# Local attention of a two-layer perceiver kernel: score matmuls ahead of the value projections, and six PSUM banks for the value projections

## The reference, cut to what matters

```python
q = h @ q_w.T + q_b
k = h @ k_w.T + k_b
v = h @ v_w.T + v_b
ph = _phrase_states(h)              # running mean within chunks of 32 tokens
pk = ph @ pk_w.T + pk_b
pv = ph @ pv_w.T + pv_b
# scores of q against the earlier k, the best 16 of them kept; score of the
# previous token's k, and of the previous token's pk; one softmax over all
w = jax.nn.softmax(all_sc, axis=-1)
out = jnp.einsum('bsn,bsnd->bsd', w, all_v)
```

## Time and profile before

| what | value |
|---|---|
| median of 3 executions | 2631.66 us |
| lowest and highest of them | 2630.71 and 2636.94 us |
| the profiled execution, its own time | 2635.64 us |
| span of its trace, first to last instruction | 2633.8 us |
| granted TensorE clock, mean over the span | 0.940 of 2.4 GHz |
| `local1` in the trace | about 2454 to 2570 us |
| `ffn1` in the trace | 2570 us to the end |

### The profile page before, as it was taken

One profiled execution on the slowest core, in us unless ns is written; L12 is line 12 of the kernel. 1 busy time (PEld: TensorE's weight loads), 2 busy tenths in 40 slices (PEclk: granted clock), 3 DMA queues, 4 the chain that ended last, 5 costly groups with the idle time before them and its releaser, 6 DMA issues. The chain is left out here.

```text
span 2633.8 us, 57280 instructions
## 1 busy us (share of the span) xinstructions
PE 2308.7 (88%) x21679; PEld 1509.7 (57%) x21955; DVE 1812.0 (69%) x3358; ACT 1574.0 (60%) x2934; POOL 1125.1 (43%) x896
## 2 busy tenths in 40 slices
PE   5389999999999999996698699995799899996885
PEld 2245665666566656665345477772567676774442
DVE  3467877888788877775164599995777777763126
ACT  3246666666666666666135399983477677886103
POOL 2245666666666665555000000004367676655000
PEclk9599999999999999998899799997899999996887
DMA  4322243224322321111531499984533334222202
GB/s 131 94 75 75 74 117 90 73 76 120 88 70 74 104 76 40 40 37 27 220 117 54 168 364 362 362 303 160 163 118 117 111 119 133 87 89 66 92 0 82
DMA packets 256290, 314.08 MB, mean 119 GB/s; under 512 B 71424, under 2 KB 182912, under 8 KB 255120
## 3 DMA queue, kind: packets, MB, share of 16 engines
q1 hardware_dynamic: 252064, 302.28, 35.7%
q10 hardware_dynamic: 3312, 6.03, 0.6%
q0 software_dynamic: 640, 2.10, 0.3%
HBM read 226.56 MB, written 48.10 MB: 104 GB/s over the span
## 5 line engine op out<-in xcount | busy, mean ns | idle before, releaser
L606 POOL TENSOR_TENSOR a_plo<-a_p,a_phi 128x512 bf16<-128x512 f32 x272 | 315.8, 1161 | 340.3 <-ACT a_phi L662 339.6
L806 PE MATMUL ps<-w_hi,a_xhi 128*128 128x512 bf16 x1086 | 412.6, 380 | 6.3
L807 PE MATMUL ps<-w_lo,a_xhi 128*128 128x512 bf16 x1086 | 412.7, 380 | 0.3 <-issue 0.2
L808 PE MATMUL ps<-w_hi,a_xlo 128*128 128x512 bf16 x1071 | 406.9, 380 | 0.1
L1978 POOL TENSOR_TENSOR a_plo<-a_p,a_phi 128x512 bf16<-128x512 f32 x256 | 306.1, 1196 | 168.5 <-ACT a_phi L2015 159.4
L628 ACT ACTIVATE a_kraw<-ps 128x256 f32<-128x256 f32 x272 | 104.2, 383 | 357.1 <-PE ps L808 355.8
L2110 DVE CUSTOM_DVE_ANT_0 a_junk<-ps,a_biasrow 128x512 bf16<-128x512 f32 x256 | 175.9, 687 | 116.0 <-PE ps L2225 90.5
L685 DVE TENSOR_TENSOR a_v<-ps,a_v 128x256 bf16<-128x256 f32 x272 | 114.1, 420 | 160.9 <-ACT a_v L630 159.5
L2010 ACT ACTIVATE a_p<-ps,a_mcol 128x512 f32<-128x512 f32 x256 | 174.8, 683 | 77.5 <-PE ps L2243 72.0
L699 DVE SCALAR_TENSOR_TENSOR a_kraw<-a_kraw,a_rn 128x1024 f32<-128x1024 f32 (+1 forms) x80 | 156.6, 1957 | 77.6 <-POOL a_rn L565 77.5
L565 POOL TENSOR_TENSOR a_rn<-a_rn,a_power 128x16 f32<-128x16 f32 (+1 forms) x80 | 204.0, 2550 | 6.7
(11 more groups left out here) (438 smaller groups left out, 6807.8 us busy)
## 6 DMA issues: line engine op xcount, KB each, us to landing
e_wst<-in_L_ffn_W SPq DMA_DIRECT2D x46, 2048.0 KB, 10.0
a_xn<-in_ctx SPq DMA_DIRECT2D x16, 1024.0 KB, 5.6
a_ks<-a_khi SPq DMA_DIRECT2D x256, 64.0 KB, 2.0
a_ks<-a_klo SPq DMA_DIRECT2D x256, 64.0 KB, 2.0
a_ct<-in_ctxT SPq DMA_DIRECT2D x16, 1024.0 KB, 6.6
a_ks<-k1h_d SPq DMA_DIRECT2D x128, 128.0 KB, 2.5
k1h_d<-a_khi SPq DMA_DIRECT2D x64, 128.0 KB, 2.0
k1l_d<-a_klo SPq DMA_DIRECT2D x64, 128.0 KB, 1.7
```

The costliest lines, as they stand in the source:

```text
L606: pool.tensor_tensor(p_lo[:, m % 3, :], p32[:, m % 2, :], p_hi[:, m % 3, :], ALU.subtract)\
L806: pe.matmul(out, x_hi[:, c, tile], w_hi[:, c, g, :], start=(c == 0), stop=False)
L807: pe.matmul(out, x_hi[:, c, tile], w_lo[:, c, g, :], start=False, stop=False)
L808: last = pe.matmul(out, x_lo[:, c, tile], w_hi[:, c, g, :], start=False, stop=(c == C - 1))
```

## The change

In `local1` the score matmuls move ahead of the value projections in the order of PE. The value projections go through six banks in the order 2, 3, 6, 7, 4, 5, 2, 3, in place of two, so that only the last two tiles have to wait for a stored one. On DVE the eight copies of value tiles, which stood ahead of the softmax, are put into it in two groups: four behind the row maximum (`m_ready`), four behind the normalised weights (`w_ready`). ACT, SP and POOL have the same instructions in the same order as before. The number of matmuls and copies is the same.

```diff
+    def bank_v(n):
+        return (2, 3, 6, 7, 4, 5)[n % 6]
...
-            for n in range(2 * B):
+
+            def value(n):
                 k, b = n // B, n % B
                 dve.wait_ge(v_mm, n + 1)
-                dve.tensor_tensor(vv[:, k, b, :], ps[:, 6 + n % 2, :], br[:, k, :], ALU.add).then_inc(v_cp, 1)
+                dve.tensor_tensor(vv[:, k, b, :], ps[:, bank_v(n), :], br[:, k, :], ALU.add).then_inc(v_cp, 1)
+
             dve.wait_ge(s_mm, 2)
...
             dve.tensor_scalar(z[:, :, 2], z[:, :, 1], -1.0, None, ALU.mult).then_inc(m_ready, 1)
-
+            for n in range(4):
+                value(n)
             step(dve.tensor_tensor(r1[:], r2[:], sc[:], ALU.not_equal))
...
             dve.tensor_tensor(wt[:, 1], sh4, per_head(z[:, :, 6], B, P), ALU.mult).then_inc(w_ready, 1)
+            for n in range(4, 2 * B):
+                value(n)
             for b in range(B):
                 dve.wait_ge(o_mm, b + 1)
...
                 last.then_inc(f_mm, 1)
-            for n in range(2 * B):
-                k, b = n // B, n % B
-                if b == 0:
-                    pe.wait_ge(w_in[3 + k], 16)
-                if n >= 2:
-                    pe.wait_ge(v_cp, n - 1)
-                for c in range(C):
-                    last = pe.matmul(ps[:, 6 + n % 2, :], (HT, PT_)[k][:, c, b * P:(b + 1) * P], w[:, 3 + k, c, :],
-                                     start=(c == 0), stop=(c == C - 1))
-                last.then_inc(v_mm, 1)
             pe.wait_ge(f_cp, 3 * C)
...
                 last.then_inc(s_mm, 1)
+            for n in range(2 * B):
+                k, b = n // B, n % B
+                if b == 0:
+                    pe.wait_ge(w_in[3 + k], 16)
+                if n >= 6:
+                    pe.wait_ge(v_cp, n - 5)
+                for c in range(C):
+                    last = pe.matmul(ps[:, bank_v(n), :], (HT, PT_)[k][:, c, b * P:(b + 1) * P], w[:, 3 + k, c, :],
+                                     start=(c == 0), stop=(c == C - 1))
+                last.then_inc(v_mm, 1)
             for k in range(2):
                 pe.wait_ge(w_ready, k + 1)
```

## The result

The changed kernel takes 2618.6 us (median of 5, 2617.03 to 2621.61) against 2631.66 us before (5, 2630.31 to 2636.94). The ratio is 0.995, its interval 0.9937 to 0.9963: 9.7 to 16.6 us faster, 13.1 by the medians. The forecast was 14.1 us and 2617.5. Measured again later, beside other kernels, the ratio was 0.9952 (0.994 to 0.9965).

The account below looks back on a forecast made before the run. The stage was taken as bound by PE, then DVE alone, then PE again. 11.4 + 0.7 + 2.5 = 14.6 us, less 0.5 for the next stage, gave 14.1 and 2617.5 us; about 9 in 10 within 2612.5 to 2624.

Parts of the forecast that it names:

- The bubble: PE ahead of the scores, now waiting for ACT's last feature copy: a new idle time, taken as 1.0 us.
- Value tiles: Eight tiles on PE behind the scores, 3.43 us each, 27.47 in all, waiting for no weights or banks.
- DVE: Softmax and value copies beside PE's value tiles: weights ready at 2536.9, wanted at 2545.0, 8.1 us of slack, softmax hidden completely.
- before all is lost: Rival that the gain does not arrive: DVE's softmax late by 8.1 us before it costs anything, 14 before all is lost; chance 0.09.
- Start of the transposes: Transposes of the weights on PE start at 2545.0 instead of 2556.43: 11.4 us earlier.
- Clock of the tail: Transposes and products of `local1` at clock 1.00 instead of partly 0.50: saves 0.7 and 2.5 us, bounds 0 and 3.2.
- The rival that the clock drops at the transposes: Products begin at low clock: gain 7.8 to 12.1 us less 0.5, time 2620 to 2624, likeliest 2621; chance 0.09.
- The next stage: Clock at the onsets of dense work in the stage behind `local1`: 0.5 us taken off the gain, bounds 0 and 1.1.
- The rival in which the clock is lost in front of the long block: Clock drops at 2510, so scores and values run low: slower, at worst 2652 us; chance 0.02.
- The rival in which the measurement hides half: Part of the rival that the gain stays within 0.3%, 7.9 us: executions differ by up to 6.2 us; 2624 to 2631; chance 0.09.

Follow-up runs that it names:

- Experiment 5: Changed kernel with value tile 0 moved ahead of the scores, into the wait for the last feature copy: `local1` 100.27 us, ratio 0.9963 to the kernel before.
- experiment 1: Changed kernel with the value tiles through two banks (6 and 7) in place of six: `local1` 103.06 us, median 2614.9 us, ratio 0.9942 to before.
- Experiment 3: Changed kernel with all eight value copies between row maximum and weights, in place of four: `local1` 109.63 us, median 2626.15 us, ratio 0.9975 to before.
- experiment 2: Changed kernel's PE order and six banks, but DVE's eight value copies ahead of the softmax as before: `local1` 117.23 us, ratio 1.0007 to before.
- Experiment 4: Kernel before with 13 extra matmuls filling PE's idle time between scores and transposes: `local1` 113.01 us, ratio 0.9981 to before.
- 6: Changed kernel, value tile 0 ahead of the scores, transposes ahead of the last tile, each product waiting for its own tiles: `local1` 99.49 us, ratio 0.9957 to before.
- experiment 7: Changed kernel with 16 extra matmuls in PE's three idle times in `ffn1`: `ffn1` 61.13 us, median 2614.42 us, ratio 0.9949 to before.
- experiment 9: As Experiment 8, but with 20 extra matmuls in `ffn1` in place of 16: `ffn1` 59.38 us, median 2613.03 us, ratio 0.9925 to before.
- Experiment 8: Changed kernel with the edits of 6 and experiment 7 together: `local1` 98.94 us, `ffn1` 60.26 us, ratio 0.9936 to before.

## Why the prediction was right

Point by point, in the order of the prediction's steps:

1. *The bubble*: taken as 1.0. Without it the scores would have begun 0.21 ahead of ACT's last copy, as the value tiles did before (2509.22 against 2509.43, rows 2 and 4), at 2504.56 - 0.21 = 2504.35; they began at 2505.30: 0.95. Experiment 5 gives 1.02 for it.
2. *Value tiles*: no wait, 27.46 us against 27.47. The banks count for 1.6 of the gain (experiment 1); the forecast had only said that none would be waited for.
3. *DVE*: slack of 8.1 us forecast and 8.1 found. Experiment 3 used it up and paid beyond it; experiment 2 shows that without this half of the change the softmax is not hidden. DVE was idle in front of tiles 2, 3, 5, 6 and 7 and of no other, as said. One figure on this slack was wrong, the 14 us of delay "before all is lost": in experiment 3 the first weights came 13.7 us later than in the changed kernel (95.55 us behind the first statistics, against 81.83), and 6.4 us of the gain were left.
4. *Start of the transposes*: 11.4 us earlier. From first statistics to transposes it is 2556.43 - 2454.43 = 102.00 before and 2540.01 - 2449.46 = 90.55 after: 11.45.
5. *Clock of the tail*: 3.2 forecast. Products begin 1.78 us after the transposes (2.66 before, 1.9 forecast) and take 2547.90 + 1.02 - 2541.79 = 7.13 (9.57 before, 7.0 forecast): 0.88 + 2.44 = 3.3. Experiment 4 gives 3.05 with the old order, so it is the clock. The rival that the clock drops at the transposes did not come true: the transposes and 0.74 us of waiting were passed at 1.00. The Trainium skill's rule (TensorE: Matmul & The Clock Gate, Part 4) that transposes do not count as activity for the clock is not tested by this run: its 1.78 us without an ordinary matmul are shorter than the 1.86 us of plain idle time that did no harm in the earlier trace rows. The earlier trace rows speak against the rule, and so does a stretch shown below this list.
6. *The next stage*: I took 0.5 off with a bound of 1.1, and the profiled pair has +1.14. It is clock: the two onsets ran low for 1.55 and 0.77 us longer, and half of the sum is 1.16. This is the term that was mis-sized. I had thought a low onset of 4.9 us the longest, and there were 5.40 and 5.04; and I took the first onset before for 3.4 from the earlier trace rows, where it is 3.85, since two records are missing at its start. Whether the longer onsets are a cost of the change stays open. Its two traces, 64.45 and 64.11, are the longest of the nine with an unedited `ffn1`; the other seven had 62.86 to 63.66, and among them are experiments 1, 3, 5 and 6, whose `local1` is shorter than before too. Experiments 7 and 9 bear out that the clock is what the stage pays for: with PE kept at work it took 61.13 and 59.38, at least 1.7 and 3.5 us under the shortest of those.

The stretch that bears on the transposes (point 5) is of the trace before, and follows the first fall of the earlier trace rows; the timeline of PE and two of its microseconds:

```profile
1400.20 5.27 PE L933 MATMUL ps<-identf,s_q 128*128 128x128 f32 x32
1403.00:1404.00 1.00, 1.00 (x8) 1.00 (x7) 0.00 (x0) 0.83 (x2) 0.00 (x0) 0.75 0.94 352
1404.00:1405.00 1.00, 1.00 (x12) 1.00 (x11) 0.00 (x0) 1.00 (x3) 0.00 (x0) 1.00 1.02 369
```

From 1399.22 to 1405.47 PE did nothing but float32 transposes (the eight of the earlier trace rows and these 32). The clock fell at about 1400.1 and rose again at about 1403.5, while they ran. For the bfloat16 transposes of `ffn1` the runs decide nothing: experiment 9 passed 3.07 us of them and their waits at 1.00, and in 7 and 8 the fall came among them.

The rival in which the clock is lost in front of the long block did not happen either. It stood at 1.00 over the values (2510 to 2540), behind a wait of 0.78 us, and experiment 1 had a further wait of 1.33 us with two banks, its 45.4 us from the scores to the products at 1.00 as well.

Terms 4 and 5, 11.45 and 3.32, make up the measured 14.77, where 14.6 was forecast. Less 1.14 in `ffn1` this is 13.6 us; the medians say 13.1, the forecast was 14.1. The interval of the times, 9.7 to 16.6 us, is too wide to test a term of 0.5 us, so that the total came close says nothing for that term. The rival in which the measurement hides half did not happen in the medians, but the profiled pair alone, 18.6 us, would have been misleading: 5 us of it lie in a stage that did not change.

## What to carry to other kernels

When an engine stands idle behind a chain on another one, look for work on it that the chain does not need, and move it behind the chain's input; and then move its consumer's instructions out of the chain on the other engine as well, into a place where there is slack. The first order alone gave nothing (experiment 2). The second alone was not run; by the program it could not work here, since PE would wait at value tile 6 for a copy that stands behind scores which it has not made. Count the clock with it: an idle time of 12 us ahead of short dense work cost 3 us more than itself. Where one execution's noise is larger than the gain, compare the length of the stage in the trace, between its barriers, not the span.

## What the runs showed of the hardware that I had not expected

- The clock can fall without a long idle time. In experiment 7 it fell at about 2564.2 (0.62 over that microsecond), and the idle times of PE ahead of it were 1.75 and 1.04 us, with 1.13 us of matmuls between. Experiment 8 had the same waits and fell 1.8 us behind the end of the second. With both filled (experiment 9) it did not fall. In the trace before, 1.86 us, 3.71 us of transposes and 1.06 us left it at 1.00. So the length of a single gap, as my prediction used it, does not decide. That gaps add up is my reading and is not shown: two traces fell and one held.
- When the clock falls varies between traces. Behind the last product of `local1` PE is idle for 11 to 12 us where `ffn1` has no edit, and the clock fell after 2.2 us in the kernel before, 3.7 and 3.2 us in the two traces of the changed one, and 4.8 us in experiment 5. So a single trace in which it held, as in experiment 9, can owe something to luck.
- Float32 transposes alone were enough for the clock to rise: it went from 0.50 to 1.00 at about 1403.5 in the trace before, while PE did nothing else (the stretch shown below the list above).
- The stage ahead of `local1` (cross attention of the second layer, with `project_back`) varied by 12 us, 630.9 to 642.6, between executions of identical code on it, while `local1` of the changed kernel varied by 0.3 in three. The cause of the 12 us stays open: no run here varied it.
